# Three mixture-of-experts stages: the second layer in three F32R passes, with hidden features split by ScalarE and GpSimd

## The chip, the cores and the metric

The kernel runs on one core of a Trainium2 chip. The metric is the time of one execution on the device in microseconds (us): the median of three timed runs, and beside it one execution that was recorded by the profiler. PE is TensorE, ACT is ScalarE, DVE is VectorE, POOL is GpSimd; PEld are TensorE's weight loads.

## What is computed

The reference is a stack of four layers, each of a cross attention and a feed-forward mixture over 2048 tokens of 128 features. The change lies in the feed-forward parts of layers 0, 1 and 2. Layer 0 (16 experts of width 128, four of them chosen per token, and one shared expert of two tiles) is

```
g = jnp.einsum('sc,ech->esh', xf, gate_w)
u = jnp.einsum('sc,ech->esh', xf, up_w)
h = jax.nn.silu(g) * u
hw = h * combine.T[:, :, None]
routed = jnp.einsum('esh,ehc->sc', hw, down_w)
return (shared_out + routed).reshape(B, T, C)
```

where `combine` holds each token's weights for its chosen experts and zero elsewhere. Layer 1 has the same form with narrower experts. Layer 2 has no second matrix: its hidden value is the square of relu of the first product. All three compute every expert for every token and weigh the result.

## The kernel before

One builder, `build_experts`, makes the stages L0f, L1f and L2f. Tokens are cut into four chunks of 512 (`CN`), features of all experts into `KC` tiles of 128: 18 in L0f, 6 in L1f, 9 in L2f. So a stage has Q = 4 KC tiles: 72, 24 and 36, and 132 in all. The first `KR` tiles of a chunk (16, 4, 8) are routed, the others belong to the shared expert and are not weighed.

A tile goes through five steps. TensorE makes its first layer (`products`, PSUM tiles `hp` and, where there are two matrices, `up`). ScalarE applies the function (`hidden`, L2757, into `g1`). VectorE multiplies (`gate`, L2928, into a ring `hid` of R = 11 buffers). For a routed tile TensorE spreads the tokens' weights over the partitions (`weigh`, L2692, into `wp`, two banks) and VectorE multiplies them in (`hidden`, L2935). TensorE then adds the second layer's product to the accumulator `yp` (`down`, L2705). After the last tile of a chunk ScalarE copies `yp` to `ft` (`finish`, L2763), TensorE turns it (`back`, L2652) and VectorE adds it to `x`.

The first layer of the first 12 or 18 tiles is plain F32; later tiles use F32R in three passes (`three`, L2656 to L2658): high part by high part, low weight by high, high weight by low. ScalarE makes the high parts of weights (L2746, L2748) and tokens (L2751); VectorE makes the low parts by subtraction (`low`, L2819 and L2822; `turn_lo`, L2827) after the loop has begun, one item in each of the first iterations: six items in L0f (the first three of two operations each), three in L1f, five in L2f. `products` of a token chunk waits for the chunk's low part. The second layer is plain F32 throughout.

Ahead of the loop stand the turning of the tokens, the router's logits, the choice of experts on VectorE (`groups` to `cast`, L2848 to L2915, with the gates of tiles 0 to 8 between) and the products of those tiles. The order on every engine is that of the code. Iteration q of the loop is, on TensorE, `products(q+9)`, `weigh(q+1)`, `down(q)`; on ScalarE `finish` of the chunk before where q starts a chunk, then `hidden(q+9)`; on VectorE `gate(q+9)`, `hidden(q+1)`, then a low part, and `finish` where q is the second tile of a chunk. GpSimd has only memsets and the tokens' reciprocal roots, all ahead of the loop.

Of the kernel before, what the change touches and what calls it, by code (L numbers as in the profile page):

```python
# [33 lines left out]
F32 = mybir.dt.float32  # L34
F32R = mybir.dt.float32r
# [2462 lines left out]
class Experts:  # L2498
# [4 lines left out]
    def __init__(self, name, E, tiles, routed, act, fill, scale, ahead, plain):  # L2503
        self.name, self.E, self.act, self.fill, self.scale = name, E, act, fill, scale
        self.KC, self.KR, self.A, self.R, self.QF = tiles, routed, ahead, ahead + 2, plain
        self.SEL = min(E, routed)
        self.share = max(1, routed // E)
        self.pieces = [(k, min(k + 6, tiles)) for k in range(0, tiles, 6)]
        self.NF = plain // tiles
        self.matrices = 2 if act == "silu" else 1  # L2510
        self.lows = [("low", i) for i in range(len(self.pieces))] + [("turn_lo", n) for n in range(self.NF, N_CHUNK)]
# [31 lines left out]
def build_experts(nc, c, io, x, x_in, x_out):  # L2543
# [6 lines left out]
    with ExitStack() as ctx, ExitStack() as done:  # L2550
# [5 lines left out]
        def sem(name):  # L2556
            sems.append(ctx.enter_context(nc.semaphore(f"{c.name}_{name}")))
            return sems[-1]
# [5 lines left out]
        w2 = sb("w2", [P, KC, P])  # L2564
# [19 lines left out]
        g1, hid = sb("g1", [P, 2, CHUNK]), sb("hid", [P, R, CHUNK])  # L2584
        ft = sb("ft", [P, CHUNK])
# [14 lines left out]
        g1_ok, gu_ok, wp_ok, hid_ok, dn_ok = [sem(n) for n in ("g1_ok", "gu_ok", "wp_ok", "hid_ok", "dn_ok")]  # L2600
        ft_ok, back_ok, xo_ok = [sem(n) for n in ("ft_ok", "back_ok", "xo_ok")]
# [26 lines left out]
        def _(pe):  # L2628
# [89 lines left out]
            weigh(0)  # L2718
            for q in range(Q):
                if q + A < Q:  # L2720
                    products(q + A)
                if q + 1 < Q:
                    weigh(q + 1)
                down(q)
                if q % KC == 1 and q >= KC:
                    back(q // KC - 1)
# [3 lines left out]
        def _(act):  # L2730
# [27 lines left out]

            def finish(n):
                act.wait_ge(dn_ok, (n + 1) * KC)  # L2760
                if n:
                    act.wait_ge(back_ok, n)
                act.activation(ft[:, :], yp[:, :], ACT.Copy).then_inc(ft_ok, 1)  # L2763
# [7 lines left out]
            for q in range(A):  # L2771
# [8 lines left out]
                if q == 3:  # L2780
                    act.wait_ge(sel_in, 16)
                    act.activation(sel[0:W, :, :], sel_f[:, :, :], ACT.Copy).then_inc(sel_ok, 1)
            for q in range(Q):
                if q % KC == 0 and q:
                    finish(q // KC - 1)
                if q + A < Q:
                    hidden(q + A)
# [3 lines left out]
        def _(pool):  # L2791
# [8 lines left out]
            for n in range(CN):  # L2800
                pool.wait_ge(mv_ok, n + 1)
                rsqrt_chunk(pool, st, half, span_of(n)).then_inc(rs_ok, 1)

        @block.vector
        def _(dve):
# [116 lines left out]
            def gate(q):  # L2922
# [3 lines left out]
                if q >= R:  # L2926
                    dve.wait_ge(dn_ok, q - R + 1)
# [51 lines left out]
            hidden(0)  # L2979
            for q in range(Q):  # L2980
                if q + A < Q:
                    gate(q + A)
                if q + 1 < Q:
                    hidden(q + 1)
# [550 lines left out]
```

## Time and profile before

| | us |
|---|---|
| median of three runs | 4478.85 (4476.98 to 4479.81) |
| the profiled execution | 4466.27 |
| its span, first to last instruction | 4464.5 |
| L0f, first normalised tile to last addition | 174 to 382 |
| L1f | 1141 to 1231 |
| L2f | 2890 to 2997 |

The profiled execution is 12.6 us shorter than the median. Times in the rows are from the span's start. A matmul row's length includes its time in the pipeline, so a pass is timed by the distance from one start to the next. One F32 matmul is written as two records.

### The profile page before, as it was taken

To read this page: it belongs to the slowest core of one execution; us is meant where nothing else is said; L and a number is where in the kernel's file an instruction comes from. 1 tells how busy PE (TensorE), PEld (TensorE's weight loads), DVE (VectorE), ACT (ScalarE), POOL (GpSimd) and SP (SyncE) were. 2 spreads that over 40 slices of the span, in tenths; PEclk is the share of its full clock that TensorE was granted. 3 is DMA by queue.
4 is the path that set the end of the run, shared out by engine and by line. 5 is a ranking of instruction groups with operands and counts; after the bars stand their busy time and mean duration, and the time that the engine had idled before them with its cause. 6 is when DMAs were issued, how large, how long until landed. Compare 5 with 4: busy or idle time off the path is not lost. (4 is left out here: it accounts for less than half of the span.)

```text
span 4464.5 us, 77156 instructions
## 1 busy us (share of the span) xinstructions
PE 4092.7 (92%) x26988; PEld 2932.2 (66%) x26988; DVE 2794.6 (63%) x6408; ACT 2798.7 (63%) x4877; POOL 810.4 (18%) x708
## 2 busy tenths in 40 slices
PE   7897999999879999999999999779999999988789
PEld 6664454454467777777777777637888888865457
DVE  7656887787565656556566665465555555548656
ACT  6423676667246666666667666526777777766457
POOL 2100000000000000000000000004777777751200
PEclk9998999999889999999999999989999999998999
DMA  2101433231010000000000000010000000000000
GB/s 73 37 1 36 70 49 45 40 42 16 13 42 1 12 12 1 13 1 12 1 13 1 12 1 1 14 36 16 8 8 1 8 8 1 1 9 1 20 23 8
DMA packets 79713, 79.34 MB, mean 18 GB/s; under 512 B 10372, under 2 KB 72996, under 8 KB 78220
## 3 DMA queue, kind: packets, MB, share of 16 engines
q1 hardware_dynamic: 73564, 67.35, 7.3%
q10 hardware_dynamic: 5760, 6.92, 0.5%
q8 instruction: 229, 3.75, 0.3%
q14 instruction: 160, 1.31, 0.1%
HBM read 51.31 MB, written 4.19 MB: 12 GB/s over the span
## 5 line engine op out<-in xcount | busy, mean ns | idle before, releaser
L2368 POOL TENSOR_TENSOR L3a_p_lo<-L3a_wq,L3a_p_hi 128x512 fp32r<-128x512 f32 (+1 forms) x480 | 617.5, 1296 | 267.7 <-ACT L3a_p_hi L2318 262.1
L1236 DVE CUSTOM_DVE_ANT_0 L2a_sc<-L2a_score,L2a_mask_n 128x804 f32<-128x804 f32 x512 | 499.2, 992 | 99.6 <-issue 76.9
L1152 ACT ACTIVATE L2a_pt<-L2a_ring 128x512 f32<-128x512 f32 x768 | 430.5, 598 | 204.9 <-PE L2a_ring L1049 203.1
L621 ACT ACTIVATE L1a_work<-L1a_ring 128x1024 f32<-128x1024 f32 x416 | 412.5, 1026 | 170.0 <-PE L1a_ring L439 168.6
L742 DVE TENSOR_REDUCE L1a_mx<-L1a_ring 128x2 f32<-128x1024 f32 x384 | 456.8, 1222 | 62.0 <-PE L1a_ring L458 58.1
L1049 PE MATMUL L2a_ring<-L2a_ident,L2a_sc 128*128 128x128 f32 x3072 | 442.5, 283 | 5.5 <-ACT L2a_sc L1139 1.9
L1139 ACT ACTIVATE L2a_sc<-L2a_sc,L2a_nb 128x1608 f32<-128x1608 f32 x256 | 417.2, 1632 | 0.7 <-DVE L2a_nb L1241 0.7
L2456 DVE TENSOR_REDUCE L3a_mx<-L3a_ring 128x1 f32<-128x402 f32 (+2 forms) x640 | 316.5, 538 | 144.2 <-PE L3a_ring L2170 136.8
L1049 PEld LDWEIGHTS L2a_ring<-L2a_ident,L2a_sc 128*128 128x128 f32 x3072 | 350.3, 144 | 79.4 <-issue 44.2
L2317 ACT ACTIVATE L3a_wq<-L3a_ring 128x512 f32<-128x512 f32 (+1 forms) x480 | 283.9, 591 | 158.5 <-PE L3a_ring L2092 103.0
L1064 PE MATMUL L2a_res<-L2a_pt,L2a_v 128*64 128x256 f32 (+1 forms) x3328 | 373.4, 381 | 1.7 <-ACT L2a_pt L1152 1.7
L1261 DVE SCALAR_TENSOR_TENSOR L2a_k_lo<-L2a_ring,L2a_bk,L2a_k_hi 128x402 fp32r<-128x402 f32 x256 | 161.3, 635 | 329.8 <-ACT L2a_k_hi L1171 328.8
L1064 PEld LDWEIGHTS L2a_res<-L2a_pt,L2a_v 128*64 128x64 f32 (+1 forms) x3328 | 233.6, 137 | 133.5 <-issue 20.3
L2792 POOL MEMSET L2f_warm<- 128x1 f32 x1 | 0.1, 99 | 1737.4 <-POOLq L64 1737.4
L2318 ACT ACTIVATE L3a_p_hi<-L3a_ring 128x512 fp32r<-128x512 f32 (+1 forms) x480 | 282.1, 588 | 0.0
L1032 PE MATMUL L2a_score<-L2a_k_hi,L2a_q_hi 64*128 64x402 f32 x1024 | 207.7, 396 | 43.9 <-DVE L2a_mx L1236 37.2
L1171 ACT ACTIVATE L2a_k_hi<-L2a_ring,L2a_bk 128x402 fp32r<-128x402 f32 x256 | 152.4, 598 | 131.4 <-PE L2a_ring L1013 128.6
L479 PE MATMUL L1a_res<-L1a_work,L1a_v 128*32 128x256 f32 (+1 forms) x3328 | 230.4, 392 | 3.2 <-ACT L1a_oraw L625 1.7
L458 PE MATMUL L1a_ring<-L1a_keys,L1a_queries 64*128 64x512 f32 (+1 forms) x1024 | 199.9, 419 | 14.8 <-DVE L1a_mx L742 13.1
L2212 PE MATMUL L3a_res<-L3a_p_hi,L3a_n_hi 128*128 128x512 f32 (+1 forms) x480 | 191.1, 398 | 16.0 <-POOL L3a_p_lo L2368 16.0
L2090 PE MATMUL L3a_ring<-L3a_q_hi,L3a_kt_hi 128*128 128x512 f32 (+1 forms) x480 | 200.2, 417 | 1.9 <-DVE L3a_q_lo L2469 1.0
L439 PE MATMUL L1a_ring<-L1a_shifted,L1a_keys 64*128 64x512 f32 x832 | 189.5, 463 | 10.9 <-issue 5.3
(754 smaller groups left out, 9077.8 us busy)
## 6 DMA issues: line engine op xcount, KB each, us to landing
L1a_keys<-L1a_k_hi SPq DMA_DIRECT2D x224, 52.0 KB
L1a_cx<-in_ctx SPq DMA_DIRECT2D x8, 768.0 KB
L2a_cx<-in_ctx SPq DMA_DIRECT2D x8, 768.0 KB
L1a_keys<-L1a_k_lo SPq DMA_DIRECT2D x112, 52.0 KB
L0a_cx<-in_ctx SPq DMA_DIRECT2D x16, 320.0 KB, 3.5
L3a_cx<-in_ctx SPq DMA_DIRECT2D x16, 320.0 KB, 3.6
L2a_mask_u<-in_mask SPq DMA_DIRECT2D x16, 200.1 KB, 4.4
L1a_scr_q<-L1a_keys SPq DMA_DIRECT2D x3, 1024.0 KB
```

Source lines behind the costliest of these rows:

```text
L479: mm = pe.matmul(res[32 * r:32 * r + 32, 0:S], v[0:rows, par, jt, h * c.VE:h * c.VE + 32], probs[0:rows, (par * NU + g * CT + jt) % c.PS, ...
L621: act.activation(probs[:, (par * NU + u) % c.PS, :, :], ring[tile][:, :, :], ACT.Exp).then_inc(tile_free[tile], 1)
L742: dve.tensor_reduce(mx[:, g % 2, hf, one, :, ch], ring[tile][:, :, :], AX, ALU.max).then_inc(tile_free[tile], 1)
L1049: mm = pe.transpose(bank[:, t * P:(t + 1) * P], sc[:, r % 2, g // 3, at:at + P], ident[:, :])
L1064: mm = pe.matmul(res[e * DH:(e + 1) * DH, 0:S], v[0:rows, t, h * DH:(h + 1) * DH], pt[0:rows, t, e, :], start=(t == 0), stop=(t == CT - 1))
L1139: act.activation(sc[:, r % 2, e, :], sc[:, r % 2, e, :], ACT.Exp, bias=nb[:, r % 2, e:e + 1], scale=1.0, accum_out=sums[:, r // 2 % 2, r % ...
L1152: ins = act.activation(pt[:, t:t + 4, g // 3, q], bank[:, :].rearrange("p (t q) -> p t q", t=4), ACT.Copy)
L1236: dve.tensor_tensor_reduce(sc[:, two, e, w].rearrange("p (k j) -> p k j", k=2), score[e][:, :, 0:CH], mask_n[:, r % 2, w].rearrange("p (k ...
L2317: act.activation(probs[0:r, at % 2, 0:W], bank[0:r, 0:W], ACT.Exp)
L2318: free(act.activation(p_hi[0:r, at % PH, 0:W], bank[0:r, 0:W], ACT.Exp), "scores", k)
L2368: pool.tensor_tensor(p_lo[0:r, at % PL, 0:W], probs[0:r, at % 2, 0:W], p_hi[0:r, at % PH, 0:W].bitcast(F32), ALU.subtract).then_inc(part_o ...
L2456: free(dve.tensor_reduce(mx[:, u % 2, part, to:to + 1], bank[:, 0:valid(s, ch)], AX, ALU.max), "tops", k)
```

## The change

The second layer becomes three F32R passes. `w2_hi` (ScalarE, L2766 in the new numbering) and `w2_lo` (GpSimd, L2829) are made in pieces of six tiles ahead of the loop, from the fifth tile on: three pieces in L0f, one in L1f, two in L2f. For each tile ScalarE copies the finished `hid` to `hid_hi` (L2775, ring of `RH` = 4) and GpSimd subtracts it from `hid` into `hid_lo` (L2833). `down` waits for that. `weigh` and VectorE's `hidden` run for tile q+3 rather than q+1 in iteration q. On ScalarE iteration q is now `hidden(q+9)`, `hidden_hi(q+2)`, and only then `finish`, which stood first before. VectorE's `gate` waits for GpSimd's reading of a buffer of the ring, not for `down`.

```diff
+        w2, w2_hi, w2_lo = sb("w2", [P, KC, P]), sb("w2_hi", [P, KC, P], F32R), sb("w2_lo", [P, KC, P], F32R)
...
-                if routed(q):
-                    pe.wait_ge(hid_ok, routed_to(q))
-                else:
-                    pe.wait_ge(gu_ok, q + 1)
-                pe.matmul(yp[:, :], w2[:, k, :], hid[:, q % R, :], start=(k == 0), stop=(k == KC - 1)).then_inc(dn_ok, 1)
+                pe.wait_ge(lo_ok, q + 1)
+                hi, lo = hid_hi[:, q % c.RH, :], hid_lo[:, q % c.RH, :]
+                pe.matmul(yp[:, :], w2_hi[:, k, :], hi, start=(k == 0), stop=False)
+                pe.matmul(yp[:, :], w2_lo[:, k, :], hi, start=False, stop=False)
+                pe.matmul(yp[:, :], w2_hi[:, k, :], lo, start=False, stop=(k == KC - 1)).then_inc(dn_ok, 1)
...
-            weigh(0)
+            for q in range(c.L + 1):
+                weigh(q)
             for q in range(Q):
                 if q + A < Q:
                     products(q + A)
-                if q + 1 < Q:
-                    weigh(q + 1)
+                if q + c.L + 1 < Q:
+                    weigh(q + c.L + 1)
                 down(q)
...
+            def hidden_hi(q):
+                if routed(q):
+                    act.wait_ge(hid_ok, routed_to(q))
+                else:
+                    act.wait_ge(gu_ok, q + 1)
+                if q >= c.RH:
+                    act.wait_ge(dn_ok, q - c.RH + 1)
+                act.activation(hid_hi[:, q % c.RH, :], hid[:, q % R, :], ACT.Copy).then_inc(hi_ok, 1)
...
+                if 5 <= q < 5 + len(c.pieces):
+                    second_hi(q - 5)
+            for q in range(c.L):
+                hidden_hi(q)
             for q in range(Q):
+                if q + A < Q:
+                    hidden(q + A)
+                if q + c.L < Q:
+                    hidden_hi(q + c.L)
                 if q % KC == 0 and q:
                     finish(q // KC - 1)
-                if q + A < Q:
-                    hidden(q + A)
...
+            for i, (p0, p1) in enumerate(c.pieces):
+                pool.wait_ge(w2_hi_ok, i + 1)
+                pool.tensor_tensor(w2_lo[:, p0:p1, :], w2[:, p0:p1, :], w2_hi[:, p0:p1, :].bitcast(F32),
+                                   ALU.subtract).then_inc(w2_lo_ok, 1)
+            for q in range(Q):
+                pool.wait_ge(hi_ok, q + 1)
+                pool.tensor_tensor(hid_lo[:, q % c.RH, :], hid[:, q % R, :], hid_hi[:, q % c.RH, :].bitcast(F32),
+                                   ALU.subtract).then_inc(lo_ok, 1)
```

TensorE's queue where the loop of L0f begins, before (`yp` in L2644 is a scratch use; L2692 weighs, L2673 and L2679 are the first layer, L2705 the second):

```order
L2644 MATMUL L0f_yp<-L0f_ident_b,L0f_cparts 128x128 x8
L2692 MATMUL L0f_wp<-L0f_ct,L0f_sel 128x512
L2673 MATMUL L0f_hp<-L0f_yt,L0f_w 128x512
L2679 MATMUL L0f_up<-L0f_yt,L0f_wu 128x512
L2692 MATMUL L0f_wp<-L0f_ct,L0f_sel 128x512
L2705 MATMUL L0f_yp<-L0f_hid,L0f_w 128x512
```

and now:

```order
L2647 MATMUL L0f_yp<-L0f_ident_b,L0f_cparts 128x128 x8
L2695 MATMUL L0f_wp<-L0f_ct,L0f_sel 128x512 x3
L2676 MATMUL L0f_hp<-L0f_yt,L0f_w 128x512
L2682 MATMUL L0f_up<-L0f_yt,L0f_wu 128x512
L2695 MATMUL L0f_wp<-L0f_ct,L0f_sel 128x512
L2706 MATMUL L0f_yp<-L0f_hid_hi,L0f_w_hi 128x512
L2707 MATMUL L0f_yp<-L0f_hid_hi,L0f_w_lo 128x512
L2708 MATMUL L0f_yp<-L0f_hid_lo,L0f_w_hi 128x512
```

Three weighings stand together ahead of the first product; with two banks of `wp` the third waits for VectorE to have taken the first.

ScalarE's queue in L0f, around the first copy of `yp` to `ft`, before:

```order
L2751 ACTIVATE L0f_yt_hi<-L0f_yt 128x512
L2757 ACTIVATE L0f_g<-L0f_hp 128x512 x20
L2763 ACTIVATE L0f_ft<-L0f_yp 128x512
L2757 ACTIVATE L0f_g<-L0f_hp 128x512 x18
L2763 ACTIVATE L0f_ft<-L0f_yp 128x512
```

and now:

```order
L2761 ACTIVATE L0f_g<-L0f_hp 128x512
L2775 ACTIVATE L0f_hid_hi<-L0f_hid 128x512
L2781 ACTIVATE L0f_ft<-L0f_yp 128x512
L2761 ACTIVATE L0f_g<-L0f_hp 128x512
L2775 ACTIVATE L0f_hid_hi<-L0f_hid 128x512
```

The copy to `ft` moved behind the function of the iteration's own product and behind a `hid_hi`.

GpSimd's queue in L0f now ends with

```order
L2533 TENSOR_SCALAR L0f_st_var<-L0f_st_mv 128x4
L2535 TENSOR_TENSOR L0f_st_rs<-L0f_st_var,L0f_half 128x4
L2533 TENSOR_SCALAR L0f_st_var<-L0f_st_mv 128x4
L2535 TENSOR_TENSOR L0f_st_rs<-L0f_st_var,L0f_half 128x4
L2829 TENSOR_TENSOR L0f_w_lo<-L0f_w,L0f_w_hi 128x768 x3
L2833 TENSOR_TENSOR L0f_hid_lo<-L0f_hid,L0f_hid_hi 128x512 x72
```

of which the last two lines are new; each of these reads two tensors in SBUF.

## Rows read from the trace of the kernel before

**Rows 1.** The page, part 1: busy time, share of the span, instructions.

```profile
PE 4092.7 (92%) x26988; PEld 2932.2 (66%) x26988; DVE 2794.6 (63%) x6408; ACT 2798.7 (63%) x4877; POOL 810.4 (18%) x708
```

**Rows 2.** Stretches: the F32R products of L0f, and those of L2f.

```profile
core 0: us, PE busy (x) PEld busy (x) DVE busy (x) ACT busy (x) POOL busy (x), PEclk, DMA share, GB/s
235.90:366.60 130.70, 130.70 (x485) 81.93 (x483) 71.22 (x104) 33.54 (x56) 0.00 (x0) 1.00 0.00 1
2935.00:2982.00 47.00, 44.53 (x146) 22.90 (x146) 32.02 (x47) 14.97 (x26) 0.00 (x0) 1.00 0.00 0
```

**Rows 3.** Timeline of TensorE, an F32R iteration of L0f: start, us, operation.

```profile
259.67 1.02 PE L2705 MATMUL L0f_yp<-L0f_hid,L0f_w 128*128 128x512 f32 x2
...
260.76 0.39 PE L2657 MATMUL L0f_hp<-L0f_yt_hi,L0f_w_lo 128*128 128x512 f32 x1
260.99 0.39 PE L2658 MATMUL L0f_hp<-L0f_yt_lo,L0f_w_hi 128*128 128x512 f32 x1
...
262.12 1.02 PE L2705 MATMUL L0f_yp<-L0f_hid,L0f_w 128*128 128x512 f32 x2
```

**Rows 4.** Timeline of TensorE, two plain F32 products of L0f in a row.

```profile
213.96 1.02 PE L2673 MATMUL L0f_hp<-L0f_yt,L0f_w 128*128 128x512 f32 x2
...
214.82 1.02 PE L2679 MATMUL L0f_up<-L0f_yt,L0f_wu 128*128 128x512 f32 x2
```

**Rows 5.** Timeline, L2f: down(3), down(26); then what `yp`'s engine waited for.

```profile
2935.21 1.02 PE L2705 MATMUL L2f_yp<-L2f_hid,L2f_w 128*128 128x512 f32 x2
...
2982.00 1.02 PE L2705 MATMUL L2f_yp<-L2f_hid,L2f_w 128*128 128x512 f32 x2
...
  DVE L2f_hid L2935: 14.7, 30
```

**Rows 6.** Timeline, L0f: ScalarE at a chunk's end, and back to back.

```profile
258.25 0.60 ACT L2763 ACTIVATE L0f_ft<-L0f_yp 128x512 f32<-128x512 f32 x1 [1.17 <-PE L0f_yp L2705]
...
261.41 0.60 ACT L2757 ACTIVATE L0f_g<-L0f_hp 128x512 f32<-128x512 f32 x1 [1.87 <-PE L0f_hp L2658]
...
199.42 0.62 ACT L2751 ACTIVATE L0f_yt_hi<-L0f_yt 128x512 fp32r<-128x512 f32 x1
...
199.94 0.59 ACT L2757 ACTIVATE L0f_g<-L0f_hp 128x512 f32<-128x512 f32 x1
```

**Rows 7.** GpSimd's subtraction in layer 3's attention: ns min/median/max.

```profile
L2368 POOL TENSOR_TENSOR L3a_p_lo<-L3a_wq,L3a_p_hi x480: 1262/1292/1480, 3048.8 to 3982.6; 128x512 fp32r<-128x512 f32 x160
```

**Rows 8.** A VectorE addition of two SBUF tensors: by tile, then beside GpSimd.

```profile
L2475 DVE TENSOR_TENSOR x_rows<-x_rows,L0a_bo x8: 405/415/427, 63.2 to 158.6; 128x256 f32<-128x256 f32 x8
L2475 DVE TENSOR_TENSOR x_rows<-x_rows,L3a_brow x8: 415/839/1281, 3090.4 to 3913.7; 128x256 f32<-128x256 f32 x8
...
3209.50 1.28 DVE L2475 TENSOR_TENSOR x_rows<-x_rows,L3a_brow 128x256 f32<-128x256 f32 x1
...
3209.22 2.72 POOL L2368 TENSOR_TENSOR L3a_p_lo<-L3a_wq,L3a_p_hi 128x512 fp32r<-128x512 f32 x2 [1.72 <-ACT L3a_p_hi L2318]
```

**Rows 9.** VectorE's subtraction with an input in PSUM, in layer 3's attention.

```profile
L2449 DVE TENSOR_TENSOR L3a_q_lo<-L3a_ring,L3a_q_hi x64: 672/692/693, 3030.5 to 3925.0; 128x512 fp32r<-128x512 f32 x64
```

**Rows 10.** Timeline, L0f: an operation of the choice, and TensorE's turning of its result.

```profile
202.08 0.43 DVE L2839 TENSOR_TENSOR L0f_run_sum<-L0f_run_sum,L0f_cnt 128x256 f32<-128x256 f32 x1
...
209.07 0.62 PE L2644 MATMUL L0f_misc<-L0f_ident_b,L0f_cparts 128*128 128x128 bf16 x8
```

**Rows 11.** Timeline, L0f: a low part of the first layer's weights.

```profile
214.55 0.95 DVE L2819 TENSOR_TENSOR L0f_w_lo<-L0f_w,L0f_w_hi 128x768 fp32r<-128x768 f32 x1
```

**Rows 12.** Timeline, L0f: down(62), the last behind a product, and the last copy.

```profile
368.65 1.02 PE L2705 MATMUL L0f_yp<-L0f_hid,L0f_w 128*128 128x512 f32 x2
...
379.50 0.60 ACT L2763 ACTIVATE L0f_ft<-L0f_yp 128x512 f32<-128x512 f32 x1 [10.98 <-PE L0f_yp L2705]
```

**Rows 13.** Stretches of TensorE alone in L1f, ahead of the loop.

```profile
1170.00:1172.00 2.00, 0.26 (x1) 1.00 0.00 0
...
1174.00:1176.00 2.00, 1.71 (x3) 0.50 0.00 0
```

More of the change, by code:

```diff
@@ L2506, in __init__ @@
         self.SEL = min(E, routed)
+        self.L, self.RH = 2, 4
         self.share = max(1, routed // E)
@@ L2563, in build_experts @@
         w1, w1_hi, w1_lo = sb("w1", [P, KC, P]), sb("w1_hi", [P, KC, P], F32R), sb("w1_lo", [P, KC, P], F32R)
-        w2 = sb("w2", [P, KC, P])
+        w2, w2_hi, w2_lo = sb("w2", [P, KC, P]), sb("w2_hi", [P, KC, P], F32R), sb("w2_lo", [P, KC, P], F32R)
         if gated:
@@ L2584, in build_experts @@
         g1, hid = sb("g1", [P, 2, CHUNK]), sb("hid", [P, R, CHUNK])
+        hid_hi, hid_lo = sb("hid_hi", [P, c.RH, CHUNK], F32R), sb("hid_lo", [P, c.RH, CHUNK], F32R)
         ft = sb("ft", [P, CHUNK])
@@ L2600, in build_experts @@
         g1_ok, gu_ok, wp_ok, hid_ok, dn_ok = [sem(n) for n in ("g1_ok", "gu_ok", "wp_ok", "hid_ok", "dn_ok")]
+        w2_hi_ok, w2_lo_ok, hi_ok, lo_ok = [sem(n) for n in ("w2_hi_ok", "w2_lo_ok", "hi_ok", "lo_ok")]
         ft_ok, back_ok, xo_ok = [sem(n) for n in ("ft_ok", "back_ok", "xo_ok")]
@@ L2696, in down @@
                 if q == 0:
-                    pe.wait_ge(w2_in, 16)
+                    pe.wait_ge(w2_lo_ok, len(c.pieces))
                     pe.wait_ge(ct_ok, 2)
@@ L2757, in hidden, with second_hi @@
                 act.activation(g1[:, q % 2, :], hp[q % NB][:, :], func).then_inc(g1_ok, 1)
+            def second_hi(i):
+                p0, p1 = c.pieces[i]
+                act.wait_ge(w2_in, 16)
+                act.activation(w2_hi[:, p0:p1, :], w2[:, p0:p1, :], ACT.Copy).then_inc(w2_hi_ok, 1)
+            def hidden_hi(q):
[6 more added lines that the diff above has]
+                act.activation(hid_hi[:, q % c.RH, :], hid[:, q % R, :], ACT.Copy).then_inc(hi_ok, 1)
             def finish(n):
@@ L2926, in gate @@
                 if q >= R:
-                    dve.wait_ge(dn_ok, q - R + 1)
+                    dve.wait_ge(lo_ok, q - R + 1)
                 dve.tensor_tensor(hid[:, q % R, :], up[q % NB][:, :], g1[:, q % 2, :], ALU.mult).then_inc(gu_ok, 1)
@@ L2978, in _ @@
             parts(1)
-            hidden(0)
+            for q in range(c.L + 1):
+                hidden(q)
             for q in range(Q):
@@ L2982, in _ @@
                     gate(q + A)
-                if q + 1 < Q:
-                    hidden(q + 1)
+                if q + c.L + 1 < Q:
+                    hidden(q + c.L + 1)
                 for kind, i in c.lows[q:q + 1]:
```

## The prediction

> **What bounds the kernel now.** I read the page's shares first, then the three stages by stretches, then the timelines of TensorE, VectorE and ScalarE in them. TensorE is busy for 92% of the span [rows 1], and in the F32R part of L0f for all of it, at the full granted clock [rows 2]. There TensorE sets the pace: one iteration is 2.45 us from one second-layer product to the next [rows 3]. A pass of F32R, from start to start, is 0.23; the two steps of a plain F32 product together take 0.86 [rows 4]. Six F32R passes (1.38), a weighing (0.23) and an F32 product (0.86) make 2.47, so nothing else is in it. L2f is another case: from down(3) to down(26) 46.8 us pass, 2.03 per iteration, where TensorE's own work (0.69 + 0.23 + 0.86) is 1.78. `yp`'s products, loads and matmuls together, find VectorE's weighed `hid` late 30 times for 14.7 us of idle time [rows 5]. VectorE reaches `hidden(q+1)` only behind `gate(q+9)`, and that waits for ScalarE and for this iteration's product.
>
> **What the passes and the longer lead give.** A second-layer product goes from 0.86 to 3 x 0.23 = 0.69 and saves 0.17. In L0f 62 iterations lie between down(0) and down(62), the last one behind a product: 10.5 us. L1f has 14 such: 2.4. In L2f the lead of three tiles lets VectorE finish about two iterations early, so I take TensorE's own work: 23 iterations of 1.38, 20 of them with a weighing of 0.23, 36.4; and two turnings of a chunk at 0.4 (the rest of L0f's 130.7 us [rows 2] over 53 iterations, six of them without a weighing, is 1.2 for three). That is 37.2 for 46.8, a gain of 9.6. Together **22.5 us**. New work beside it: per tile ScalarE 0.5 and GpSimd 1.29 [rows 6, 7], both below the new pitch (2.3 in L0f, 1.6 in L2f); `hid_lo` is ready 0.6 us or more ahead of its product in L2f, over two in L0f.
>
> **The chunk's end.** `finish` now stands behind `hidden(q+9)` and `hidden_hi(q+2)`. `hidden(q+9)` waits for the iteration's own product: its function starts 0.42 after the start of the third pass (260.99 to 261.41 [rows 3, 6]), so 0.89 after the iteration's first. ScalarE's operations follow each other by about 0.5 (199.42 to 199.94 [rows 6]), so the copy starts at 1.89, ends at 2.49, and TensorE goes on at 2.54. It would have been ready at 1.61 in L0f and L1f and at 0.92 in L2f. Before, the copy at 258.25 was done long ahead. The wait is 0.93 at three ends in L0f and two in L1f, 1.62 at two in L2f (the last ends of L1f and L2f have no product ahead of them): **7.9 us** lost.
>
> **The loop's start.** The third weighing waits until VectorE has used the first bank (`hidden(0)`, 0.69). TensorE stands for about 0.85 us and does two weighings (0.46) early that it gets back only in the tail, where others bound it. down(0) comes 1.3 later, in each stage: **4.0 us** with 1.4 in L2f, where VectorE's low part of the tokens then comes that much later.
>
> **The tail.** The last nine tiles have no products. Before, TensorE and VectorE alternate; from down(62) to the last copy pass 10.85 us [rows 12]. Now GpSimd is the slowest link: in L0f lo(65) starts 2.2 after down(62) (the gate, `hidden(65)`, its high part), and seven at 1.285 end at 11.2, the copy starts at 12.1: **1.3 us** lost. In L1f and L2f the tail of before has a copy to `ft` inside and is longer; the same count comes out within 0.5 of it, and I take nothing.
>
> **GpSimd against VectorE.** This term decides. An addition of two SBUF tensors on VectorE takes 0.415 while GpSimd is idle (layer 0, at most 0.427). In layer 3, beside GpSimd's subtractions, the same takes up to 1.28 [rows 8]. At 3209.50 it starts 0.28 after a subtraction of 1.28 and ends 0.28 after that one's end: it stood until GpSimd was through, and the pair of subtractions took 2.72 where two take 2.57. VectorE's subtraction with an input in PSUM never exceeds 0.693 in the same stage [rows 9]. So `gate` and `hidden`, which read PSUM, are safe, and the operations of the choice and the low parts, which read two SBUF tensors, are not. The Trainium skill says the same of its cause: "SBUF — State Buffer", section "SBUF: two separate sides", has the pair of ports that both use as an exclusive lock for the whole instruction, whichever starts first, and VectorE takes it with two SBUF inputs. By that rule the long `w2_lo` operation would hold VectorE for all of its length; the longest wait that a row shows is 0.87 (1.28 - 0.415), and with six times 0.87 in place of the 8.8 below the sum would be 1.5 rather than 5.2. The rule is borne out as far as the rows reach.
>
> *Ahead of the loop.* A `w2_lo` of 768 columns is 1.5 x 1.285 = 1.93 us. In L0f the first piece is ready on ScalarE about 201.8, in the middle of the choice, where VectorE is the last to be waited for (TensorE turns its result at 209.07 [rows 10]). The operation of 202.08 waits until about 203.95 and loses 1.7, the next again 1.7 behind the second piece, the third piece costs 1.4: 4.8. L1f has one piece, 1.4; L2f one of 1.93 and one of 0.97, 2.6. Sum **8.8 us**, at least 0 and at most 10.8 (5.8 + 1.9 + 2.9, plus issue).
>
> *In the first iterations.* VectorE there also makes low parts, 0.95 each and two per iteration in L0f [rows 11], while GpSimd now runs once per iteration. Its iteration is 3.3 us alone; with one or two waits of 0.9 to 1.3 it becomes 4.2 to 5.2 against TensorE's 2.6. Followed through, TensorE waits for gate(11) and gate(12) by 1.8 each in L0f, 3.6; in L1f products(12) wait 1.7 for the tokens' low part; in L2f 0.4. Sum **5.7 us**, from 0 to 14.
>
> **The sum.** -22.5 + 7.9 + 4.0 + 1.3 + 8.8 + 5.7 = +5.2. The profiled execution of 4466.27 becomes 4471.5; the median lies 12.6 above it, so I forecast 4478.85 + 5.2 = **4484** us. By stages: L0f +3, L1f +4, L2f -2.
>
> **Rivals.** *The two engines do not hold each other here* (as four of the eight additions of layer 3 at 0.415 show, that is a matter of meeting). Then 14.5 fall away: -9.3, 4469.5. Against it: GpSimd has an operation in every iteration, and the pieces of `w2` come due in the choice itself. Chance 0.13. *The holding costs its full price:* each of the 18 low-part operations (9, 4, 5) loses a whole 1.285 and the pieces their full length. VectorE's first three iterations in L0f are then 5.9, it falls 12 behind, TensorE can run ahead some 5, and stands 7 rather than 3.6; L1f and L2f add 1.5 each, the pieces 1.8: +13.4, 4492. It becomes slower than measurement can miss from 3.8 us over my sum. For it: GpSimd's subtraction starts at once when ScalarE is done, and VectorE is continuous there. Also for it, TensorE's clock: in L1f its granted clock is 1.00 (2.4 GHz) while it is busy for 0.26 of 2 us, and 0.50 (1.2 GHz) from 1174 [rows 13]; longer idle times could bring more such stretches. Chance 0.22. *ScalarE is not late at a chunk's end*, because something else holds the product anyway: up to 7.9 back, 4476. Chance 0.07. *The change does not do what it says:* three passes with loads between take the 0.86 of before. 99 iterations at 0.17 are 16.8, giving 4501. The first layer's own passes speak against it. Chance 0.03.
>
> **How the numbers follow.** My forecast has the remaining 0.55. About 0.2% (9 us) is what a measurement of this kernel can tell from no change. Faster by more than that holds only the first rival and a little of mine, 0.12; slower the second, the last and the top of mine, 0.25; within it 0.63. The range of 8 in 10 takes in the first two rivals with 1.5 us to spare: 4468 to 4494.
>
> **What would show it.** Right: L2705's three successors 0.23 apart; an iteration of 2.3 us in L0f and 1.6 in L2f; `ft` behind a `hid_hi`, and TensorE's wait on `ft` of 0.9 and 1.6; VectorE operations of the choice at 2 us instead of 0.43 beside `w2_lo`, and TensorE's turning of the weights 5 us later in L0f; GpSimd without gaps in the tail. Wrong: VectorE's two-input operations at their old lengths (then the first rival); many of over 2 us in the first ten iterations (then the second); GpSimd's `hid_lo` well over 1.3 us, which would make it the pace of L2f, 36 tiles long.

## The result, and the profile after

Timed on the same chip (15 runs of each), the kernel before took 4478.44 us and the changed one 4488.87, both medians; the ratio is 1.0021, 95% interval 1.0012 to 1.0030. The change costs 0.21%, 9.4 us by the ratio (the two medians are 10.4 apart). A second series (d0 below) gave 1.0021 again, interval 1.0007 to 1.0036. The forecast was +5.2 us. One execution of a2 below took 7168.6 us and is in none of the ratios.

The profiled executions are 24.6 us apart (spans 4464.5 and 4489.1), and most of that isn't the change. Between VectorE's clearing of `seg` and the end of the last copy to `ft`, the three changed stages take 414.5 us before and 420.6 after; what lies outside takes 4050.0 and 4068.5. Over all thirteen profiled executions of this study that outside part, the same code each time, ranges from 4050.0 to 4076.3 in no order that a change would explain (the changed kernel again: 4062.8). So the whole span tells little here, and the stages' inner landmarks tell much: between runs of the same code they repeat within some 0.1 us, apart from the stretches ahead of the loop, where TensorE's granted clock varies. In L0f the first row of the table takes 8.90 to 8.91 with the clock at full (before, a2, c1, d1), and 9.47 to 9.58 where it is at half for 3.4 us (a3, b3, d2), with no subtraction on GpSimd there in any of the seven. Those I use:

| us | L0f before, after | L1f before, after | L2f before, after |
|---|---|---|---|
| first operation of the last choosing to the turning of the weights | 8.90, 13.24 | 9.80, 10.28 | 9.13, 11.47 |
| turning to down(0) | 4.03, 5.28 | 3.85, 5.29 | 4.38, 5.63 |
| down(0) to the last product with a first-layer product ahead | 155.55, 151.85 | 35.21, 36.51 | 54.62, 51.56 |
| from there to the start of the last copy to `ft` | 10.85, 12.21 | 12.46, 11.76 | 13.25, 14.18 |

The sum of the differences is +7.2. L0f's 8.90 has the full clock; the changed kernel takes 13.23 or 13.24 there with 3.4 us or 6.8 us at half. Against 9.5 the sum would be 6.6. What the rows of after show, in the order of the prediction. The page's shares, to set beside [rows 1]; VectorE's timeline in the choice of L0f, where the addition of [rows 10] is the third row; then GpSimd's there (start us, duration, engine, line, operation, names, shapes; idle time in front and its releaser in brackets):

```profile
PE 4095.5 (91%) x27084; PEld 2970.6 (66%) x27120; DVE 2809.6 (63%) x6408; ACT 2871.9 (64%) x5015; POOL 988.7 (22%) x846
```

```profile
201.48 0.42 DVE L2868 TENSOR_REDUCE L0f_cnt<-L0f_above 128x16 f32<-128x256 f32 x1
201.82 0.68 DVE L2869 TENSOR_TENSOR_SCAN L0f_run_sum<-L0f_seg,L0f_equal 128x256 f32<-128x256 f32 x1
202.58 1.87 DVE L2871 TENSOR_TENSOR L0f_run_sum<-L0f_run_sum,L0f_cnt 128x256 f32<-128x256 f32 x1
204.52 1.86 DVE L2873 SCALAR_TENSOR_TENSOR L0f_equal<-L0f_run_sum,L0f_equal 128x256 f32<-128x256 f32 x1
206.46 0.42 DVE L2875 TENSOR_TENSOR L0f_comb<-L0f_above,L0f_equal 128x256 f32<-128x256 f32 x1
...
211.60 1.88 DVE L2945 TENSOR_TENSOR L0f_comb<-L0f_comb,L0f_cparts 128x256 f32<-128x256 f32 x1
```

```profile
202.35 3.75 POOL L2829 TENSOR_TENSOR L0f_w_lo<-L0f_w,L0f_w_hi 128x768 fp32r<-128x768 f32 x2 [21.43 <-ACT L0f_w_hi L2766]
211.29 1.91 POOL L2829 TENSOR_TENSOR L0f_w_lo<-L0f_w,L0f_w_hi 128x768 fp32r<-128x768 f32 x1 [5.19 <-ACT L0f_w_hi L2766]
```

Three operations of 0.42 take 1.87: each starts inside a subtraction of GpSimd and ends some 0.3 after that one's end. This is the holding that the prediction called the deciding term, and it is longer here than the 0.87 that a row of before showed: the wait has the length of what is left of GpSimd's operation. It also catches VectorE's low parts at the loop's start, which were 0.95 in [rows 11], and TensorE then waits:

```profile
222.25 2.04 DVE L2854 TENSOR_TENSOR L0f_wu_lo<-L0f_wu,L0f_wu_hi 128x768 fp32r<-128x768 f32 x1
226.46 2.05 DVE L2854 TENSOR_TENSOR L0f_wu_lo<-L0f_wu,L0f_wu_hi 128x768 fp32r<-128x768 f32 x1
...
229.16 1.13 PE L2676 MATMUL L0f_hp<-L0f_yt,L0f_w 128*128 128x512 f32 x2 [1.18 <-DVE L0f_hid L2960]
...
233.39 1.13 PE L2676 MATMUL L0f_hp<-L0f_yt,L0f_w 128*128 128x512 f32 x2 [1.33 <-DVE L0f_hid L2960]
```

The second layer's passes (beside [rows 3]), 2.31 from one tile to the next, and the first product of a new chunk on TensorE and what ScalarE did ahead of it:

```profile
261.13 0.58 PE L2706 MATMUL L0f_yp<-L0f_hid_hi,L0f_w_hi 128*128 128x512 f32 x1
261.55 0.39 PE L2707 MATMUL L0f_yp<-L0f_hid_hi,L0f_w_lo 128*128 128x512 f32 x1
261.78 0.40 PE L2708 MATMUL L0f_yp<-L0f_hid_lo,L0f_w_hi 128*128 128x512 f32 x1
...
263.44 0.58 PE L2706 MATMUL L0f_yp<-L0f_hid_hi,L0f_w_hi 128*128 128x512 f32 x1
...
266.87 0.50 PE L2706 MATMUL L0f_yp<-L0f_hid_hi,L0f_w_hi 128*128 128x512 f32 x1 [1.00 <-ACT L0f_ft L2781]
```

```profile
265.22 0.60 ACT L2761 ACTIVATE L0f_g<-L0f_hp 128x512 f32<-128x512 f32 x1 [1.19 <-PE L0f_hp L2661]
265.71 0.62 ACT L2775 ACTIVATE L0f_hid_hi<-L0f_hid 128x512 fp32r<-128x512 f32 x1
266.23 0.59 ACT L2781 ACTIVATE L0f_ft<-L0f_yp 128x512 f32<-128x512 f32 x1
```

In L2f the same wait is 1.48. The tail of L0f on GpSimd, without a gap between seven subtractions, 1.25 each; and stretches of L2f, the later three behind the wait for the tokens' low part (the figures behind the busy times are the granted clock, the DMA share and GB/s), where [rows 2] had 1.00 from 2935 on. The first line is from the loop's start, just behind down(0):

```profile
373.46 8.73 POOL L2833 TENSOR_TENSOR L0f_hid_lo<-L0f_hid,L0f_hid_hi 128x512 fp32r<-128x512 f32 x7 [0.48 <-ACT L0f_hid_hi L2775]
```

```profile
2946.00:2948.00 2.00, 2.00 (x6) 1.53 (x5) 1.17 (x2) 1.12 (x2) 1.63 (x2) 0.50 0.00 0
2953.00:2957.00 4.00, 2.99 (x10) 2.17 (x10) 2.22 (x4) 1.11 (x2) 1.10 (x2) 0.79 0.00 0
2957.00:2961.00 4.00, 4.00 (x15) 2.73 (x13) 3.70 (x6) 2.23 (x4) 1.78 (x2) 0.79 0.00 0
2961.00:2965.00 4.00, 4.00 (x18) 2.91 (x19) 3.02 (x5) 2.79 (x6) 3.52 (x3) 1.00 0.00 0
```

### The profile page after: what moved, and what is told of

Its sections match the earlier page's. It is cut to its first block and busy times, and to the rows that moved or that the text cites. A ratio compares the mean times of both kernels' runs of the same rounds, so it can differ in the third digit from the quotient of the medians.

```text
span 4489.1 us, 77792 instructions
## 1 busy us (share of the span) xinstructions
PE 4095.5 (91%) x27084; PEld 2970.6 (66%) x27120; DVE 2809.6 (63%) x6408; ACT 2871.9 (64%) x5015; POOL 988.7 (22%) x846
```

## The experiments

Eleven runs, in three series; each series was timed against the kernel before on its own chip. b2 and d1 are one execution each, read by their rows and landmarks alone. Ratios are to that. All stage times are between the landmarks of the table, and "loop" is from down(0) to the start of the last copy to `ft` (before 166.4, 47.67, 67.87; changed 164.06, 48.27, 65.74).

**a1: the copy to `ft` first.** On ScalarE:

```
             for q in range(Q):
+                if q % KC == 0 and q:
+                    finish(q // KC - 1)
                 if q + A < Q:
                     hidden(q + A)
                 if q + c.L < Q:
                     hidden_hi(q + c.L)
-                if q % KC == 0 and q:
-                    finish(q // KC - 1)
```

> The changed kernel with one edit: ScalarE copies the finished chunk to ft as the first step of its iteration again, ahead of hidden(q+9) and hidden_hi(q+2). Measured against the changed kernel's own stages, from VectorE's clearing of seg to the end of the last copy to ft: 214.75 us in L0f, 93.65 in L1f, 112.20 in L2f. My theory (the copy is late because it stands behind two operations of ScalarE that wait for the iteration's own product): the waits on ft go, 3 x 1.12 in L0f, 2 x 0.9 in L1f and 2 x 1.49 in L2f, so the stages take about 211.4, 91.9 and 109.2, together 8.2 less. Rival (something else holds the chunk's first product, the low part by GpSimd or the turning back): under 4 us less, and another name stands as releaser in front of that product.

Measured: ratio 0.9997 (0.9985 to 1.0009). Loops 160.97, 46.15, 61.81: 3.1, 2.1 and 3.9 less. Whole stages are 211.4, 93.0 and 108.3, 7.9 less for the 8.2 expected. From one chunk to the next L0f goes from 42.65 to 41.62 and L2f from 16.60 to 14.98, so an end cost 1.03 and 1.62. The rival falls. ScalarE and TensorE at a chunk's end of L2f now:

```profile
2957.41 0.58 ACT L2781 ACTIVATE L2f_ft<-L2f_yp 128x512 f32<-128x512 f32 x1
2957.99 0.60 ACT L2761 ACTIVATE L2f_g<-L2f_hp 128x512 f32<-128x512 f32 x1
...
2958.04 0.50 PE L2706 MATMUL L2f_yp<-L2f_hid_hi,L2f_w_hi 128*128 128x512 f32 x1
```

**a2: no `w2_lo`.** GpSimd zeroes the tensor at the stage's start and gives the signal:

```
-                pool.tensor_tensor(w2_lo[:, p0:p1, :], w2[:, p0:p1, :], w2_hi[:, p0:p1, :].bitcast(F32),
-                                   ALU.subtract).then_inc(w2_lo_ok, 1)
+                pool.nop().then_inc(w2_lo_ok, 1)
```

> The changed kernel without GpSimd's subtractions that make w2_lo: the tensor is set to zero at the stage's start, and only the signal is given (so the low part of the second layer's weights is left out of the result). My theory (a GpSimd subtraction of two SBUF tensors stops VectorE's operations with two SBUF inputs for as long as it runs): the operations of the choice at 1.87, 1.86 and 1.88 in L0f, and the scan at 1.81 in L1f, are back at 0.42 and 0.68, and the turning of the weights comes 4.4 earlier in L0f, 1.1 in L1f, 2.3 in L2f; the stages take about 210.4, 92.5 and 109.9. Rival (GpSimd and VectorE do not stop each other; the three long operations are a slower form of the same work, or the chunk's parts are waited for anyway): the long operations stay and the stages are within 1 us of the changed kernel's.

Measured: from the last choosing to the turning 8.91, 9.83, 9.12, as before the change (4.33, 0.45 to 0.76 and 2.35 less than with it; the middle one depends on which level TensorE's clock has there). The addition is back:

```profile
205.12 0.43 DVE L2871 TENSOR_TENSOR L0f_run_sum<-L0f_run_sum,L0f_cnt 128x256 f32<-128x256 f32 x1
205.62 0.43 DVE L2873 SCALAR_TENSOR_TENSOR L0f_equal<-L0f_run_sum,L0f_equal 128x256 f32<-128x256 f32 x1
```

The whole stages (213.0, 95.0, 111.0) came out 1.1 to 2.6 us above what I expected, and the ratio is 1.0000 (0.9988 to 1.0013): with the zeroing that I had put into GpSimd's queue the stage's start, up to the first operation of the choice (VectorE's addition into `choice`), is 0.7 to 2.0 us longer, in a4 as well. The landmarks behind it aren't touched.

**a4: no `hid_lo`**, in the same manner, in the loop.

> The changed kernel without GpSimd's subtractions in the loop that make hid_lo: the ring is set to zero at the stage's start and only the signal is given (the low part of hid is left out of the result). My theory: VectorE's low parts in the first iterations are back at 0.95 from up to 2.05, TensorE's two waits there in L0f (1.18 and 1.33) and the one for the tokens' low part in L1f (1.54) go, and so does GpSimd's pace in the tail (1.24 per tile): L0f 3.0 and 1.4 less (210.4), L1f 1.5 less and up to 1 in the tail (91.5), L2f 0.5 less at the loop's start and 0.9 in the tail; and if the stretch of L2f at half clock (2955 to 2958.6) comes of the wait of 2.29 us ahead of it, another 1.5 there. Sum 7 to 9. Rival (low parts are late because of ScalarE's additional copies, not because of GpSimd): the waits of L0f stay, and only the tails get shorter, 2 to 3 us in all.

Measured: ratio 0.9994 (0.9981 to 1.0007); loops 157.22, 44.62, 62.03, so 6.8, 3.7 and 3.7 less, 14.2 in all against the 7 to 9 expected. TensorE's waits in L0f went as expected. The first copy to `ft` comes 2.9, 1.7 and 2.6 earlier; the 2.6 of L2f isn't GpSimd's alone, since TensorE's clock also differs there (below). The low part is short beside an idle GpSimd:

```profile
230.44 0.95 DVE L2851 TENSOR_TENSOR L0f_w_lo<-L0f_w,L0f_w_hi 128x768 fp32r<-128x768 f32 x1
231.30 0.95 DVE L2854 TENSOR_TENSOR L0f_wu_lo<-L0f_wu,L0f_wu_hi 128x768 fp32r<-128x768 f32 x1
232.17 0.68 DVE L2960 TENSOR_TENSOR L0f_hid<-L0f_up,L0f_g 128x512 f32<-128x512 f32 x1
```

Most of the surplus is in the tails, 7.0 us shorter in all where 3.3 was expected: L0f 8.3 us in place of 12.2. I had reckoned it back to the tail of before (10.85), where a product takes 0.86 and the lead is short, but three passes with a lead and no GpSimd are quicker than either.

**a3: the lead alone**, in the kernel before, second layer in plain F32:

```
-            weigh(0)
+            for q in range(c.L + 1):
+                weigh(q)
...
-                if q + 1 < Q:
-                    weigh(q + 1)
+                if q + c.L + 1 < Q:
+                    weigh(q + c.L + 1)
```

and the same for VectorE's `hidden`.

> The kernel before with the longer lead alone (weighing three tiles ahead on TensorE and VectorE), the second layer in plain F32 as before: no high and low parts, nothing on GpSimd. Stages of before: 211.35, 92.43, 110.76. My theory: the loop starts 1.25 later in each stage; in L0f nothing comes back outside the tail; in L2f VectorE is not late any more and an iteration is TensorE's own 1.79 with a weighing, 1.56 without, in place of 2.03: 23 of them 5.8 less. So +1.3, +1.3 and -4.5 without the tails, which may be up to 2 us shorter each, since the weighed tiles are ready earlier; whole kernel 0 to 6 us less than before. Rival (in L2f the pace of 2.0 is set by gate and ScalarE, not by the lead): L2f stays at 2.0 per iteration and is 1.3 longer, and the gain of the changed kernel in L2f is the passes' alone.

Measured: ratio 0.9987 (0.9976 to 0.9998); loops 165.19, 45.56, 60.58. L2f's loop is 7.3 shorter than before, which is over three times what the whole change brings there (2.1). From one chunk to the next it takes 16.30 in place of 18.38. Ahead of it down(0) comes 5.16, 5.16 and 5.99 behind the turning (before 4.03, 3.85, 4.38); the 5.99 has TensorE's clock at half all the way. TensorE has no wait left in such an iteration, 1.81 from product to product, what its work adds up to:

```profile
2957.53 1.05 PE L2706 MATMUL L2f_yp<-L2f_hid,L2f_w 128*128 128x512 f32 x2
2958.02 0.79 PE L2657 MATMUL L2f_hp<-L2f_yt_hi,L2f_w_hi 128*128 128x512 f32 x1
2958.65 0.39 PE L2658 MATMUL L2f_hp<-L2f_yt_hi,L2f_w_lo 128*128 128x512 f32 x1
2958.88 0.40 PE L2659 MATMUL L2f_hp<-L2f_yt_lo,L2f_w_hi 128*128 128x512 f32 x1
2959.12 0.39 PE L2693 MATMUL L2f_wp<-L2f_ct,L2f_sel 128*128 128x512 bf16 x1
2959.34 1.02 PE L2706 MATMUL L2f_yp<-L2f_hid,L2f_w 128*128 128x512 f32 x2
```

**b1: the third weighing behind the first product**, on top of a1:

```
-            for q in range(c.L + 1):
+            for q in range(c.L):
                 weigh(q)
             for q in range(Q):
                 if q + A < Q:
                     products(q + A)
+                if q == 0:
+                    weigh(c.L)
```

(VectorE's `hidden` likewise.)

> The changed kernel with two edits: ft copied first in ScalarE's iteration (as in a1), and the third weighing, with its hidden(2) on VectorE, placed behind the first product of the loop instead of ahead of it. Theory (TensorE stands about 0.85 us ahead of the loop because the third weighing waits for VectorE to free a bank): from the turning of the weights to down(0) in L0f and L1f it takes 4.4 to 4.5 in place of 5.28 and 5.10 to 5.29; in L2f, where down(0) waits for GpSimd's first low part, less comes back, 0 to 0.8. The rest of the loop as in a1: from down(0) to the end 160.97, 46.15 and 61.8. Rival (down(0) is held by GpSimd's chain of high part and low part in all three stages): unchanged within 0.2.

Measured: turning to down(0) 5.27, 5.10, 5.55. Here my theory fell. The stand ahead of the third weighing is gone and another takes its place: in L0f down(0) waits for GpSimd.

```profile
221.85 0.47 PE L2706 MATMUL L0f_yp<-L0f_hid_hi,L0f_w_hi 128*128 128x512 f32 x1 [0.65 <-POOL L0f_hid_lo L2835]
```

So two causes of equal lateness lay one behind the other. a4, which takes away only GpSimd's part, gives 5.14 in L0f; only b3, without either (and with the second layer in plain F32), brings it back. L2f can't be read like this, because TensorE's clock is at half there. a4 has 4.57 for 5.63, but its clock is back at full 1.5 us ahead of down(0); in the changed kernel it stays at half beyond it, the product ahead takes 1.71 where it takes 0.86 at full, and down(0) follows without a wait, 0.2 after GpSimd has made its low part. In b2, with the clock back 2.1 us ahead, down(0) waits for GpSimd and still comes at 5.56:

```profile
2941.84 0.47 PE L2706 MATMUL L2f_yp<-L2f_hid_hi,L2f_w_hi 128*128 128x512 f32 x1 [0.64 <-POOL L2f_hid_lo L2832]
```

So in L2f the low clock and GpSimd's chain make down(0) equally late. Loops in b1 are 160.73, 45.50 and 61.85, so L0f and L1f are 0.2 and 0.7 shorter than in a1. Ratio 1.0000 (0.9986 to 1.0014).

**b2: a copy for the subtraction of `w2_lo`.**

> The changed kernel with GpSimd's subtraction for w2_lo replaced by a plain copy of w2 of the same columns (one input in SBUF; the low part is then wrong and the second layer's result with it). Theory A (any GpSimd operation on SBUF holds VectorE's two-input operations): the copy takes as long as the operation of VectorE beside it is lengthened, and choice operations of well over 0.43 us remain, at least one for each piece. Theory B (only GpSimd's operation with two tensor inputs holds VectorE): they are back at 0.42 and 0.68 although GpSimd is busy; from the first operation of the last choosing to the turning it is then 8.90 in L0f in place of 13.24.

Measured: 9.91 from the last choosing to the turning in L0f. That figure alone decides little, since with the clock as low as it was here a3, b3 and d2 take 9.5 to 9.6 without any such work. The rows decide: GpSimd's copy is shorter (0.82 to 1.06 for the subtraction's 1.81 to 1.97) but holds VectorE all the same, even a conversion of VectorE with a single input (0.29 otherwise). Theory A, though not for each piece: at the second, VectorE's operation started 0.05 earlier, kept its 0.43, and the copy took 1.06. GpSimd's first and third piece, then VectorE:

```profile
202.34 0.82 POOL L2829 CAST L0f_w_lo<-L0f_w 128x768 fp32r<-128x768 f32 x1 [22.46 <-ACT L0f_w_hi L2766]
...
208.57 0.83 POOL L2829 CAST L0f_w_lo<-L0f_w 128x768 fp32r<-128x768 f32 x1 [3.44 <-ACT L0f_w_hi L2766]
```

```profile
202.58 0.87 DVE L2870 TENSOR_TENSOR L0f_run_sum<-L0f_run_sum,L0f_cnt 128x256 f32<-128x256 f32 x1
...
208.79 0.76 DVE L2946 CAST L0f_cparts<-L0f_comb 128x256 bf16<-128x256 f32 x1
```

**b3: the lead alone, third weighing behind the first product.**

> The kernel before with the longer lead alone, second layer in plain F32 (as a3), with the third weighing behind the first product of the loop. From the turning to down(0) 4.3 to 4.4 in L0f and L1f in place of a3's 5.16; from down(0) to the end about as a3: 165.2, 45.6, 60.6. Whole stages: sum of the three loops with their starts about 10.6 less than before, less 2 times 0.25 for the two weighings made early: the kernel 8 to 11 us faster than before. If the third weighing's wait was hidden anyway: as a3.

Measured: ratio 0.9982 (0.9967 to 0.9996), 8 us faster than before, as expected; turning to down(0) 4.29, 4.28, 4.50; loops 165.19, 45.57, 60.78.

**c1: a version from the findings.** b3, with ScalarE's copy first, and the three passes only where they pay:

```
+        self.split = range(*{'L0f': (12, 63), 'L1f': (0, 0), 'L2f': (10, 27)}[name])
...
+                if q not in c.split:
+                    if routed(q):
+                        pe.wait_ge(hid_ok, routed_to(q))
+                    else:
+                        pe.wait_ge(gu_ok, q + 1)
+                    pe.matmul(yp[:, :], w2[:, k, :], hid[:, q % R, :], start=(k == 0), stop=(k == KC - 1)).then_inc(dn_ok, 1)
+                    return
...
-                if 5 <= q < 5 + len(c.pieces):
-                    second_hi(q - 5)
...
+                if c.split and 0 <= q - c.split[0] + 5 < len(c.pieces):
+                    second_hi(q - c.split[0] + 5)
+                if q + c.L in c.split:
                     hidden_hi(q + c.L)
```

> A version put together from the findings: the longer lead in all three stages, the third weighing behind the first product, ft copied first; the second layer in three passes only for tiles 12 to 62 of L0f and 10 to 26 of L2f, the others and all of L1f in plain F32; w2's parts are made in the loop, where VectorE makes no low parts any more. Theory: from the first operation of the last choosing to the turning 8.9 in L0f and 9.1 in L2f, as before; VectorE's operations with two SBUF inputs all at their short lengths; L0f from down(0) to the end 165.2 (lead alone) less 51 x 0.157 = 157.2; L1f 45.6; L2f 60.6 less 17 x 0.17 = 57.7. Against before (166.4, 47.67, 67.87) 21.4 less, 0.5 of it given back by early weighings: the kernel 17 to 21 us faster, ratio 0.9955 to 0.9963. Rival (VectorE, ScalarE or GpSimd is the pace of L2f at 1.62 per iteration, so that the passes give nothing there; switching between the two kinds costs more than a pass): L2f stays near 60.6 and the sum is 12 to 15.

Measured: ratio 0.9963 (0.9948 to 0.9978), 16.6 us faster than before, just short of the 17 to 21 expected. Loops 157.26, 45.56, 58.20; from the last choosing to the turning 8.90, 9.74, 9.13. The first is what the sum said, 157.2; L2f got 2.6 of 2.9 from the passes. The rival falls. The addition of the choice, and `w2_lo`, which GpSimd now makes from 232.77 on, behind VectorE's last low part:

```profile
201.25 0.43 DVE L2881 TENSOR_TENSOR L0f_run_sum<-L0f_run_sum,L0f_cnt 128x256 f32<-128x256 f32 x1
```

```profile
232.77 1.81 POOL L2839 TENSOR_TENSOR L0f_w_lo<-L0f_w,L0f_w_hi 128x768 fp32r<-128x768 f32 x1 [53.00 <-ACT L0f_w_hi L2778]
```

**d0: the changed kernel again.**

> The changed kernel itself once more, on the same chip as the two below. If its stages are what the first profile showed, they are again 164.06, 48.27 and 65.7 us from down(0) to the end, and 13.24, 10.3 to 10.6 and 11.47 from the last choosing to the turning; the kernel 5 to 11 us slower than before. If the part of the first difference that lay outside the three stages (18.5 us between the two profiled executions) belongs to the change, this run's other stretches are as long as in the first profile; if it is how executions vary, they differ from it by several us.

Measured: ratio 1.0021 (1.0007 to 1.0036). Loops 164.03, 48.23, 65.86; 13.23, 10.59 and 11.46 ahead. The outside part is 4062.8, 5.7 less than in the first profile of the same code. So several us of the first difference are how executions vary; one repeat can't show that all of it is.

**d1: three passes in the tail too** (`(12, 72)` and `(10, 36)`).

> The combined version with one edit: three passes up to the last tile (12 to 71 in L0f, 10 to 35 in L2f) in place of 12 to 62 and 10 to 26. Theory (in the tail GpSimd's subtraction, 1.24 us per tile, is the slowest link; in plain F32 it is TensorE's 1.07): from down(62) to the end 12.2 in L0f, as in the changed kernel, in place of 9.68, so the loop is 159.8 instead of 157.26; L2f about 1.2 to 1.6 longer than 58.20. Rival (the tail is bound by the weighing, whichever way the second layer is made): within 0.5 of the combined version.

Measured: loops 159.77 and 59.91, against 157.26 and 58.20. GpSimd is the tail's pace, and plain F32 is the quicker way there:

```profile
363.00 8.71 POOL L2843 TENSOR_TENSOR L0f_hid_lo<-L0f_hid,L0f_hid_hi 128x512 fp32r<-128x512 f32 x7 [0.48 <-ACT L0f_hid_hi L2787]
```

**d2: c1 again.**

> The combined version once more, beside the changed kernel. Its stages should again be 157.26, 45.56 and 58.20 from down(0) to the end; against before the kernel is 13 to 21 us faster, and against the changed kernel above 22 to 30 us.

Measured: ratio 0.9946 (0.9927 to 0.9965), 24 us faster; against the changed kernel beside it, 4454.94 and 4489.60, 35 us. Both are above what I expected (13 to 21, 22 to 30), from six executions. Loops 157.30, 45.54, 58.14; from the last choosing to the turning 9.58, 9.80, 9.13, the first with the clock at half for 3.4 us. The two series bracket what the stages show, 18 to 20 us (394.9 and 396.4 for 414.5).

## Why the prediction was right

Its sum was +5.2; the landmarks give +7.2 and the timing 9.4 (5.4 to 13.4). The mechanisms that it named are there, with one left out: it put TensorE's clock in L2f at nothing, and that was worth 2.8 us. Term by term, with the experiment that bears on it; the first line is what remains when the others are taken off, not a measurement of its own:

| term | predicted | measured | from |
|---|---|---|---|
| passes and longer lead | -22.5 | -21.1 | difference of down(0) to the last covered product, less the two terms that lie in it |
| chunk's end | +7.9 | +8.4 | a1: 3 x 1.03, 2 x 1.06, 2 x 1.62 |
| loop's start | +4.0 | +3.9 | table; b1, b3 |
| tail | +1.3 | +1.6 | table; d1 |
| holding ahead of the loop | +8.8 | +7.2 (6.6 against L0f's 9.5) | table; a2 |
| holding in the first iterations, with 2.8 of TensorE's clock in L2f | +5.7 | +7.2 | a4: 2.9, 1.7, 2.6 |

**Passes and lead.** A tile saves 0.16 rather than 0.17 in L0f (2.31 for 2.47), 9.7 for 10.5; L1f 2.5 for 2.4; L2f 8.9 for 9.6. The prediction didn't part the lead from the passes, and a3 does: in L2f three fifths of the gain per chunk are the lead's (18.38 to 16.30 in a3, to 14.98 with the passes in a1), and it needs no high or low parts.

**Chunk's end.** Right in cause and size. It was the cheapest mistake of the change: a1 takes it back with a reordering.

**Loop's start.** Right in size, half wrong in cause. I put the 1.3 down to the third weighing alone; b1 shows GpSimd's first low part equally late. Mending only the one gained nothing (b1), mending only the other 0.1 in L0f (a4).

**Tail.** L0f +1.36 as predicted. The others weren't nothing: L1f -0.7, L2f +0.9. They nearly cancel, which is luck.

**Holding ahead of the loop.** The deciding mechanism is there, with the full length of GpSimd's operation, as the Trainium skill has it ("SBUF — State Buffer", section "SBUF: two separate sides"); the other reading that the prediction weighed, at most 0.87 per meeting, is refuted by the 1.86 to 1.88 above. (By that reading the prediction's sum is 1.6, not 1.5.) L0f cost 4.34 for 4.8, or 3.7 against the kernels with the low clock, and L2f 2.34 for 2.6. L1f was mis-sized, 0.5 to 0.8 for 1.4: the scan that is held (1.81 for 0.68) loses 1.13, and 0.37 of that falls on an idle time in which VectorE had waited for TensorE's last product before the turning. An operation that ran in the middle of the same subtraction, with one input, isn't held:

```profile
1176.68 2.02 POOL L2829 TENSOR_TENSOR L1f_w_lo<-L1f_w,L1f_w_hi 128x768 fp32r<-128x768 f32 x1 [19.06 <-ACT L1f_w_hi L2766]
...
1177.10 0.42 DVE L2868 TENSOR_REDUCE L1f_cnt<-L1f_above 128x16 f32<-128x256 f32 x1
1177.44 1.81 DVE L2869 TENSOR_TENSOR_SCAN L1f_run_sum<-L1f_seg,L1f_equal 128x256 f32<-128x256 f32 x1
```

**Holding in the first iterations.** L0f 2.9 for 3.6 and L1f 1.7 for 1.7. L2f came out at 2.6 for 0.4, and what is in it isn't the holding but TensorE's clock, which the prediction had in a rival and in no term. Twice the clock is at half where a4 has it at full. First at the loop's start: it fell at 2931.4, ahead of the turning, as it does in L2f in all thirteen profiled executions, and is back at 2948.5, 2.5 us behind down(0) (2.7 behind in d0, 1.5 ahead in a4, just ahead in the kernel before). So down(1) follows down(0) after 2.97 where a4 has 1.77, 1.2 more. Changed kernel, then a4:

```profile
2945.93 0.99 PE L2706 MATMUL L2f_yp<-L2f_hid_hi,L2f_w_hi 128*128 128x512 f32 x1
...
2948.91 0.59 PE L2706 MATMUL L2f_yp<-L2f_hid_hi,L2f_w_hi 128*128 128x512 f32 x1
```

```profile
2933.31 0.58 PE L2706 MATMUL L2f_yp<-L2f_hid_hi,L2f_w_hi 128*128 128x512 f32 x1
...
2935.08 0.58 PE L2706 MATMUL L2f_yp<-L2f_hid_hi,L2f_w_hi 128*128 128x512 f32 x1
```

Then again from about 2955.3 to 2958.7: down(4) and down(5) follow after 2.62 and 2.16 where a4 has 1.63 and 1.58, 1.6 more. Together that is 2.8, and from down(1) to down(3) the changed kernel is even 0.2 shorter than a4. What the holding takes in L2f with the clock at full shows in a1, from down(0) to the end of TensorE's wait for the tokens' low part: 7.45 there, 7.04 in a4, so 0.4, as predicted. Six profiled executions show the second fall (the changed kernel's two, a1, a2, b1, b2), all those with both three passes and GpSimd's low parts from the first tile; the other seven (before, a3, a4, b3, c1, d1, d2) don't. TensorE's idle time just ahead doesn't part them: 2.28 to 2.87 us with the fall, 1.40 to 2.45 without. What brings it about, and what sets when the first one ends, stays open.

The two holding terms add up to 14.4 for a predicted 14.5. That is partly luck: without the clock's 2.8 they are 11.6, and the clock was in no term.

**The rivals.** No holding (-9.3): refuted by a2 and a4. Full price (+13.4): the timing alone, 9.4 with 13.4 at the end of its interval, can't tell it from the forecast, and its sign, low parts of over 2 us, is there three times in L0f (2.04 to 2.06). The rows refute it all the same: of the six low parts of weights in L0f four are held, by 0.7 to 1.1, and the tokens' there not at all. ScalarE not late: refuted by a1. Passes no quicker: refuted, 2.31. The prediction's bound of 0.2% for what can be told from no change was met almost exactly by the result, 0.21%: the forecast lay on the near side of it and the time on the far one, with an interval that reaches to both sides.

## What to carry to other kernels

Work moved to GpSimd isn't free for VectorE even where GpSimd is idle: look at what VectorE runs at that moment, and put the work where VectorE reads from PSUM; c1 and d2 do nothing else with `w2_lo` in L0f and L2f, leave it out in L1f, and have 6.5 to 7.5 us back ahead of the loop. Test the parts of a change apart: of one with three parts (a lead, a cheaper product, helpers for it), the lead alone was worth more than the whole, and the cheaper product paid only in the middle of a long loop, away from its start and its tail. A step that waits for its own iteration's product belongs behind whatever others wait for. And where two causes are late together, take both away before judging either. An experiment that takes work away can also move TensorE's clock, as a4 did in L2f: set the granted clock of both runs beside each other before a gain is put down to the work.

## What the runs showed of the hardware

- VectorE's operation with two inputs in SBUF that starts while GpSimd's runs lasts until that one's end and then most of its own time (0.28 of 0.42, 0.81 of 0.95): 0.42 becomes 1.86 to 1.95 beside a subtraction of 768 columns, 0.87 beside a copy of 0.82. Such a held operation has a long row and no idle time in front, so no list of waits shows it.
- GpSimd's plain copy holds it as well, and VectorE's conversion from F32 to BF16 with one input is held too (0.29 to 0.76). The same section of the Trainium skill counts operations in a two-port mode among those that take the lock; the trace agrees as far as this one row goes, and no row tells in which mode the conversion ran. A TENSOR_REDUCE with one input isn't held (0.42 inside a subtraction of 2.02, above). Its operations with an input in PSUM never were: the 244 gates and weighings of the three changed stages take at most 0.694.
- It goes both ways. At the loop's start of L0f in b1, two of GpSimd's subtractions take 4.01 in place of 2.51 (the two before them), while VectorE's low parts lie between (line L2835, then VectorE):

```profile
223.88 4.01 POOL L2835 TENSOR_TENSOR L0f_hid_lo<-L0f_hid,L0f_hid_hi 128x512 fp32r<-128x512 f32 x2 [0.93 <-ACT L0f_hid_hi L2777]
```

```profile
223.84 0.95 DVE L2853 TENSOR_TENSOR L0f_w_lo<-L0f_w,L0f_w_hi 128x768 fp32r<-128x768 f32 x1
224.70 2.04 DVE L2856 TENSOR_TENSOR L0f_wu_lo<-L0f_wu,L0f_wu_hi 128x768 fp32r<-128x768 f32 x1
```

- In all thirteen executions TensorE's clock is at half from before the turning in L2f, and what follows depends on when it is back: from down(0) to down(1) 2.97 or 1.77 with the same work on TensorE (after, a4).
- The same code outside the three stages took 4050 to 4076 us in thirteen executions. A difference of 0.2% can't be read from the spans of two profiles.
